# Gram lower triangles: a side of a group takes every other pair of batches, one 16,128-byte run per lane, and 4-lane stores in every fourth group

## The reference

```python
def setup_inputs(...):
    r_inputs = -4.11716e-05 + 1 * jax.random.normal(..., (2048, 64, 256), jnp.float32)

def reference(inputs):
    Z = jnp.einsum('bnd,bmd->bnm', inputs, inputs)
    n = inputs.shape[1]
    li, lj = jnp.tril_indices(n, k=-1)
    return Z[:, li, lj]
```

## Time and profile before

| | us |
|---|---|
| median of 3 runs | 401.72 (401.25 to 402.3) |
| the profiled execution, its own time | 403.43 |
| its span | 401.6 |
| PE busy | 365.2 (91%) |
| DVE busy | 362.3 (90%) |
| ACT busy | 178.4 (44%) |
| POOL busy | 197.7 (49%) |
| DMA, queue of SP / of ACT, share of 16 engines | 83.8% / 9.6% |

### The profile page before, as it was taken

One profiled execution on the slowest core, in us unless ns is written; L12 is line 12 of the kernel. 1 busy time (PEld: TensorE's weight loads), 2 busy tenths in 40 slices (PEclk: granted clock), 3 DMA queues, 4 the chain that ended last, 5 costly groups with the idle time before them and its releaser, 6 DMA issues.

```text
span 401.6 us, 68674 instructions
## 1 busy us (share of the span) xinstructions
PE 365.2 (91%) x33024; PEld 359.8 (90%) x33024; DVE 362.3 (90%) x240; ACT 178.4 (44%) x821; POOL 197.7 (49%) x974
## 2 busy tenths in 40 slices
PE   4439999999999999999999999998999899998960
PEld 4439999999999999999999999998989899998960
DVE  3417899999999999999999998989999798998995
ACT  0011224555445544465445654453554344455463
POOL 1000047282833866086817475283835738184585
PEclk9999999999999999999999999999999999999995
DMA  8299999999999999999999999999999999998417
GB/s 319 105 351 427 420 422 423 420 405 421 422 425 402 422 425 421 422 415 425 420 424 413 421 417 419 352 399 417 381 425 360 425 370 422 403 366 339 138 31 206
DMA packets 21274, 151.01 MB, mean 376 GB/s; under 512 B 2688, under 2 KB 2816, under 8 KB 4864
## 3 DMA queue, kind: packets, MB, share of 16 engines
q1 hardware_dynamic: 18752, 135.77, 83.8%
q10 hardware_dynamic: 2496, 14.97, 9.6%
HBM read 134.22 MB, written 16.52 MB: 375 GB/s over the span
## 4 chain that ended last, share of the span: by engine, by line
DVE 43%; DMA 34%; issue 13%; PE 8%; DVEq 0%
DVE x_turned L233 38%; DMA x_in<-x_dram 34%; PE bank_set L311 8%; DVE row_halves L250 3%; DVE x_in L257 1%; DVE packed_rows L153 1%; DVE packed_rows L142 0%; DVE x_turned L262 0%; DVEq L249 0%; DVEq L232 0%; DVEq L74 0%; DVEq L282 0%
## 5 line engine op out<-in xcount | busy, mean ns | idle before, releaser
L311 PE MATMUL bank_set<-x_turned 32*64 32x64 f32 x33024 | 365.2, 237 | 23.3 <-issue 15.1
L311 PEld LDWEIGHTS bank_set<-x_turned 32*64 32x64 f32 x33024 | 359.8, 132 | 28.5 <-issue 16.1
L233 DVE STREAM_TRANSPOSE x_turned<-x_in 128x2048 f32<-128x2048 f32 x128 | 287.9, 2280 | 33.8 <-PE bank_set L311 18.4
L153 POOL COPY packed_rows<-row_halves 32x32 f32<-32x32 f32 (+30 forms) x930 | 190.0, 204 | 198.3 <-DVE row_halves L250 98.6
L342 ACT COPY products<-bank_set 128x512 f32<-128x512 f32 (+1 forms) x91 | 68.4, 758 | 153.1 <-PE bank_set L311 141.0
L250 DVE STREAM_TRANSPOSE row_halves<-products 128x1024 f32<-128x1024 f32 x60 | 72.2, 1205 | 0.0
L142 ACT COPY packed_rows<-row_halves 128x32 f32<-128x32 f32 (+30 forms) x465 | 61.4, 220 | 16.6 <-DVE row_halves L250 16.5
L148 ACT COPY packed_rows<-row_halves 128x128 f32<-128x128 f32 x240 | 54.0, 299 | 27.8 <-DMA y_dram<-packed_rows 16.1
L342 ACT ACT_TABLE_LOAD x1 | 1.3, 1283 | 19.6 <-PE bank_set L311 19.6
L153 POOL COPY packed_rows<-x_in 32x32 f32<-32x32 f32 (+30 forms) x31 | 4.9, 209 | 0.1
L257 DVE STREAM_TRANSPOSE x_in<-products 128x512 f32<-128x512 f32 (+1 forms) x5 | 4.8, 998 | 0.0
## 6 DMA issues: line engine op xcount, KB each, us to landing
x_in<-x_dram SPq DMA_DIRECT2D x128, 1024.0 KB, 16.2
y_dram<-packed_rows ACTq DMA_DIRECT2D x22, 504.0 KB, 9.2
y_dram<-packed_rows ACTq DMA_DIRECT2D x6, 252.0 KB
y_dram<-packed_rows ACTq DMA_DIRECT2D x24, 63.0 KB
y_dram<-packed_rows SPq DMA_DIRECT2D x2, 504.0 KB, 4.7
y_dram<-packed_rows SPq DMA_DIRECT2D x1, 380.0 KB
y_dram<-packed_rows ACTq DMA_DIRECT2D x1, 380.0 KB
y_dram<-packed_rows SPq DMA_DIRECT2D x1, 124.0 KB
```

Source lines behind the costliest of these rows:

```text
L153: return copy(packed_rows[first:first + BLOCK, group % 2, :, at + BLOCK:at + i], halves(group)[first + BLOCK:first + HALF, i, :, 0:i - BLOCK])
L233: nc.vector.transpose(x_turned[:, j].rearrange("p c b s (h u n v) -> p u v (c b s h) n", h=ROWS // BLOCK, u=PAIRS, v=PAIR), x_in[:, k]).th ...
L311: done = nc.tensor.matmul(bank_sets[s][side * HALF:(side + 1) * HALF, g, at, :].rearrange("r (n u v) -> r u n v", u=PAIRS, v=PAIR), rows, ...
```

## The change

Within a quadrant the batch is now `2*side + slot` in place of `2*slot + side`: side and slot change places in the layout of `x_turned`, and in the order in which PE takes them. In groups 0 to 14, ACT's copy to `products` puts slot b in half b: the batch of a group becomes `q*4 + side*2 + h`. A lane's two triangles are then neighbours in DRAM, and its store is one run of 16,128 bytes. ACT's copy writes its elements in turns to two places 32 floats apart, where it wrote 8 or 16 in a row.

The last group keeps its halves of four tiles, with batch `h*64 + q'*4 + side*2 + b` for lane `b*16 + q'`. Its lanes are stored 16 at a time (`HALF_SIDES`), so that each of its four DMAs of before is two. The groups with 4-lane DMAs are 1, 5 and 9, where they were 1, 3, 5, 7, 9 and 11; groups 3, 7 and 11 are stored whole.

```diff
-        x_turned = sbuf("x_turned", [PARTS, LAP, CHUNKS, SLOTS, SIDES, ROWS])
+        x_turned = sbuf("x_turned", [PARTS, LAP, CHUNKS, SIDES, SLOTS, ROWS])
...
+    HALF_SIDES = [[(side, q, q + BLOCK // SLOTS) for q in range(0, BLOCK, BLOCK // SLOTS)] for side in range(SIDES)]
...
-            return group % 2 == 1 and group <= FEW_UNTIL
+            return group % 4 == 1 and group <= FEW_UNTIL
...
-            rows = y[group * GROUP:(group + 1) * GROUP, columns].rearrange("(h q s) c -> s q h c", h=RUNS, s=SIDES)
+            rows = y[group * GROUP:(group + 1) * GROUP, columns]
             for side, first, end in lanes:
-                engine.dma_start(rows[side, first:end],
-                                 packed_rows[side * HALF + first:side * HALF + end, group % 2, :, columns]).then_inc(
-                    stored[group % 2], 16)
+                packed = packed_rows[side * HALF + first:side * HALF + end, group % 2, :, columns]
+                if group < GROUPS - 1:
+                    to = rows.rearrange("(q s h) c -> s q h c", s=SIDES, h=RUNS)[side, first:end]
+                else:
+                    to = rows.rearrange("(h q s b) c -> s b q h c", h=RUNS, s=SIDES, b=SLOTS)[side, first * SLOTS // BLOCK]
+                engine.dma_start(to, packed).then_inc(stored[group % 2], 16)
...
-            store(engine, group, slice(long_rows, PACKED), WHOLE_SIDES[side:side + 1])
+            store(engine, group, slice(long_rows, PACKED), HALF_SIDES[side])
...
-            store(engine, group, slice(0, long_rows), WHOLE_SIDES[side:side + 1])
+            store(engine, group, slice(0, long_rows), HALF_SIDES[side])
...
-                                rows = x_turned[g * BLOCK:(g + 1) * BLOCK, j, c, slot, side]
+                                rows = x_turned[g * BLOCK:(g + 1) * BLOCK, j, c, side, slot]
...
+                    to = products[:, group % KEPT_RING]
+                    if group < GROUPS - 1:
+                        to = to.rearrange("p i (b t g) -> p i t g b", b=RUNS, g=QUADRANTS)
+                    else:
+                        run = in_group // (GROUP_TILES // RUNS)
+                        to = to.rearrange("p i (r b t g) -> p r i t g b", r=RUNS, b=SLOTS, g=QUADRANTS)[:, run]
+                        in_group %= GROUP_TILES // RUNS
                     last = nc.scalar.copy(
-                        products[:, group % KEPT_RING, :, in_group * PER_SIDE:(in_group + count) * PER_SIDE].rearrange(
-                            "p i (m g b) -> p i m g b", g=QUADRANTS, b=SLOTS),
+                        to[:, :, in_group:in_group + count],
```

More of the change, by code:

```diff
@@ L196, in _ @@
             for b in range(2):
-                last = 2 * len(WHOLE_SIDES) * 16 if (GROUPS - 1) % 2 == b else 0
+                last = 2 * sum(map(len, HALF_SIDES)) * 16 if (GROUPS - 1) % 2 == b else 0
                 sync.wait_ge(stored[b], stores_before(GROUPS + b) + last)
@@ L233, in turn @@
                 nc.vector.transpose(
-                    x_turned[:, j].rearrange("p c b s (h u n v) -> p u v (c b s h) n", h=ROWS // BLOCK, u=PAIRS, v=PAIR),
+                    x_turned[:, j].rearrange("p c s b (h u n v) -> p u v (c s b h) n", h=ROWS // BLOCK, u=PAIRS, v=PAIR),
                     x_in[:, k]).then_inc(turned[j], LAP)
```

## The result

The changed kernel takes 410.33 us (median of 6 runs, 409.24 to 412.23), the kernel before beside it 402.04 (401.25 to 403.02). The ratio is 1.0213, 95% interval 1.0182 to 1.0244: **8.3 us slower**, where 5.7 us faster was forecast and the slowest of the rivals with a price stood at 406.3.

What follows compares the result with a forecast made beforehand. One late DMA engine, slow on stores beside loads, was taken to bound the second half; -8.5 (long runs and thinning) + 2.0 (waits that stay) + 0.8 (end) = -5.7 us, giving 396.0 us; range 392.8 to 406.3 with a little room.

Steps and rivals of the forecast that it cites:

- the slowest of the rivals with a price: Rival A: long store runs crowd out loads in the mixed phases, 406.3 us; chance 0.33 together with rival B.
- What bounds the kernel: Second half: one late DMA engine, none of the 4-lane four, pays 0.55 us per store run where others take 0.31.
- Fewer groups with 4-lane DMAs: Groups 3, 7 and 11 stored whole: 6 more runs of 8064 bytes on the last engine, +3.3 us.
- Runs of 16,128 bytes: Stores of groups 0 to 14: fewer runs on the last engine, -8.5 us including the +3.3 of thinning.
- the excess of 0.24 us: Late engine's store runs beside loads: 0.55 us each against 0.31 on others, taken as all per run.
- both ends, -8.5 and +3.3: Late engine's stores, thinning included: -8.5 us if all excess is per run, +3.3 if cost is by bytes.
- an argument about the ordinary engines: Mixed phases: ordinary engines pay by bytes at 426 GB/s, so one engine's excess looks like run handling or load/store changes.
- rival B: Late engine's excess is by bytes: +3.3 from thinner 4-lane scheme, +0.8 at end, 405.8 us; chance 0.33 with rival A.
- rival A: Mixed phases: long store runs crowd out loads, +3.8 us, with the end 406.3 us; chance 0.33 together with rival B.
- ACT's copy: Copies from PSUM: at most doubled to 1.87 and 1.01 us, hidden from PE, so no change to the sum.
- The end: Last group's stores: +0.4 us for one issue more, +0.4 for 16 lanes of a side drawn at once, +0.8 in all.
- The range: Whole kernel: from rival D's 392.8 us to rival A's 406.3, each with a little room.

Runs made afterwards that it cites:

- the dealings: Kernel before with side 1's store lanes in groups 0 to 12 split otherwise (none, 30/2, 16/8/8, 7/7/2, 5/5/5/1, eight 4-lane groups): ratios 1.0223, 1.019, 1.062, 1.0487, 1.0652, 1.0063.

## Why the prediction was wrong, point by point

**What bounds the kernel: right.** One engine that isn't among the four of the 4-lane stores sets the pace of the second half. It was inferred from the stretch 376 to 378 and the count of runs, and the dealings confirm it. That all of its excess lies on stores was the simplest reading, and the packet records put most of it on the loads between them.

**Fewer groups with 4-lane DMAs: the sign and place right, the size at most a little short.** It was +3.3 by the forecast and +4.3 measured, with 3.3 inside the interval. With 12 runs more, 0.55 us each would be 6.6, and 9.0 was measured (7.7 to 10.2). The 0.55 us came from two waits 16 tiles apart; the marginal price is nearer 0.7. Why a further run costs more than the mean one is open.

**Runs of 16,128 bytes: this is the step that failed.** The sum took all of the excess of 0.24 us as a cost per run that halves with the number of runs, -8.5 us with the thinning in it. The runs showed a cost by bytes in its place: with half the runs the last load lands at 380.84 where the forecast had 373, and the time is +1.4 us where it had -8. The prediction had both ends, -8.5 and +3.3, and chose by an argument about the ordinary engines, which says nothing on what slows one engine alone. With no row between two ends 12 us apart and on both sides of zero, the likelier sign was not known; rival B had the right mechanism, and its signs came: an unchanged rate in the mixed phases, and waits of DVE at 14.6 us where it had 13. Its time, 405.8, was 4.5 us short. That the long runs themselves would cost 1.4 us was in rival A's direction and far below its 3.8; the mixed phases move at 424 GB/s as before (window 142 to 146 of the changed kernel, for before), so nothing crowded loads out there, while long runs alone (1.4 us) remain unexplained:

```profile
142.00:146.00 4.00, 4.00 (x400) 4.00 (x391) 4.00 (x3) 1.90 (x2) 2.95 (x15) 1.00 1.01 424
```

**ACT's copy: size nearly right, cover wrong at one place.** They doubled, 2.06 and 1.10 us where 1.87 and 1.01 stood as the upper bound, and they are hidden as far as PE is concerned: no wait of PE for ACT appears. But the cover was worked out for PE alone. In the last group DVE has no tile left to transpose and waits for the copy itself. Alone the copies cost 0.7 us of the median and a wait of 1.3 us in the trace. In the changed kernel the wait is 2.1 us, and the 0.8 us between fit the clock granted to PE after it had stood idle, which the prediction didn't have.

**The end: a term too small.** It was +0.8 by the forecast and +2.2 measured alone. Each extra DMA was priced at an issue of 0.4 us; one issue on each queue took 2.30 us, and the rate of the last stores fell from 211 to 144 GB/s.

**The range.** It took each rival with its own term and the same small end. The end and the copies (2.9 us together) were on top of rival B, and no case had them all.

## What to carry to other kernels

When one of many equal engines is late, first find out by what it is charged, with one dose up and one down, before sizing a change that lowers the number of its jobs but not their bytes. An uneven distribution that looks like a nuisance may be what spares it: ask who would get the work back. And a cover that holds in the middle of a pipeline has to be checked again for the last group, where the engine that waited for loads waits for whatever comes next.

## What the runs showed of the hardware

One of the 16 DMA engines, the fifth if a DMA of few lanes always takes the first ones, costs the kernel 0.55 to 0.75 us for each further 8064 bytes that it stores to DRAM beside loads, where 0.31 is the time of such a packet on the others, on all three chips of the runs. In the trace of before its loads between stores take about 0.5 us, and its stores 0.34 to 0.39. Loads alone don't show it: there a load follows every 2.49 us, with the late engine among those that it waits for. The Trainium skill ("DMA: Bandwidth & Descriptors", Latency and other measured facts) calls engines 7 and 15 usually slower. Counted from 0 these are the eighth and the last, and in this case neither is the one. Why it is the fifth, and only with stores among its loads, is open.
